# A graph transformer with linear attention and a mixture of experts on one core: the join of nodes that cross tiles multiplies in two reduced-precision parts, and the first attention's one-hots and slot gathers change their places in the queues

## The reference, cut to what matters

```python
for l in range(2):
    q = ((x @ Wq[l].T + bq[l]) * scaling).reshape(n, H, DH)      # H = 8, DH = 64
    k = (x @ Wk[l].T).reshape(n, H, DH)
    v = (x @ Wv[l].T).reshape(n, H, DH)
    scores = einsum('ehd,ehd->eh', q[tgt], k[srcidx])
    p = exp(scores - segment_max(scores, tgt)[tgt])
    w = p / (segment_sum(p, tgt)[tgt] + 1e-16)
    agg = segment_sum(w[:, :, None] * v[srcidx], tgt)
    x = batchnorm(x + agg.reshape(n, D) @ Wo[l].T + bo[l])
    x = batchnorm(x + relu(x @ W1[l].T + b1[l]) @ W2[l].T + b2[l])
```

## Time and profile before

| what | us |
|---|---|
| median of 3 runs | 3262.51 (3260.45 to 3280.92) |
| the profiled execution | 3271.22 |
| span of its instructions | 3269.9 |
| first attention, PE at work in it | about 508 to 1350 |
| first join, L1697 to the read back | 1381.5 to 1420.7 |
| second attention | about 1825 to 2507 |
| second join's matmuls | 2535.5 to 2565.8 |

### The profile page before, as it was taken

How to read it: one execution, slowest core, us unless ns; L and a number is a source line. 1 busy time by engine, 2 the same in 40 slices (tenths; PEclk the granted TensorE clock), 3 DMA queues, 4 the chain that set the end, 5 groups by cost and what they waited for, 6 DMA issues and landing times.

```text
span 3269.9 us, 78219 instructions
## 1 busy us (share of the span) xinstructions
PE 2847.2 (87%) x32206; PEld 1996.0 (61%) x32206; DVE 1677.8 (51%) x3300; ACT 1270.2 (39%) x3609; POOL 1098.5 (34%) x1109
## 2 busy tenths in 40 slices
PE   6999997999989998677799799889886785899998
PEld 5877875666666666355488566666664462444444
DVE  5237774555454544535513355555555357555554
ACT  3324444455544544212332355555554112222221
POOL 0000004666666555200001477777773001111100
PEclk8999998999999999788899899999998897899999
DMA  6542007888888888521024699999996221011100
GB/s 210 221 153 89 30 30 249 296 306 303 299 295 296 292 290 280 147 68 59 30 98 150 218 353 351 345 351 353 347 347 203 62 85 39 26 39 39 48 32 15
DMA packets 223590, 608.82 MB, mean 186 GB/s; under 512 B 37008, under 2 KB 43792, under 8 KB 223219
## 3 DMA queue, kind: packets, MB, share of 16 engines
q0 software_dynamic: 137088, 466.78, 40.6%
q1 hardware_dynamic: 86131, 136.85, 12.5%
HBM read 525.96 MB, written 103.29 MB: 192 GB/s over the span
## 4 chain that ended last, share of the span: by engine, by line
PE 66%; DMA 16%; DVE 6%; issue 6%; POOL 4%; ACT 2%; SPq 1%; POOLq 0%; DVEq 0%; ACTq 0%
PE ps L1106 8%; DMA stage<-Qd,segs 7%; PE ps L2320 5%; PE ps L1129 5%; PE ps L2341 5%; PE ps L555 4%; DMA Y<-KVd,srcE 4%; PE ps L556 4%; PE ps L557 4%; PE ps L1141 3%; PE ps L915 3%; PE ps L620 2%; PE ps L622 2%; PE ps L621 2%; PE ps L1697 2%
## 5 line engine op out<-in xcount | busy, mean ns | idle before, releaser
L1026 POOL DMA_INDIRECT Y<-KVd,srcE x449 | 438.1, 976 | 146.2 <-issue 107.0
L1106 PE MATMUL ps<-ident,Y 128*128 128x128 f32 x1796 | 287.1, 283 | 38.0 <-DMA Y<-KVd,srcE 30.5
L1301 ACT ACTIVATE stage<-ps,stage 128x128 f32<-128x128 f32 x832 | 293.2, 372 | 22.5 <-DVE stage L1213 20.6
L1026 POOL DMA_INDIRECT WA<-KVd,srcE x186 | 182.0, 979 | 330.9 <-PE ps L557 267.0
L1282 ACT ACTIVATE G<-ps 128x512 f32<-128x512 f32 x315 | 188.7, 600 | 255.5 <-PE ps L1106 254.4
L1282 ACT ACTIVATE work<-ps 128x512 f32<-128x512 f32 x309 | 185.6, 601 | 241.5 <-PE ps L1106 239.6
L555 PE MATMUL ps<-Wh,xs 128*128 128x512 f32 x600 | 238.8, 398 | 38.0 <-DVE xs L495 38.0
L1106 PEld LDWEIGHTS ps<-ident,Y 128*128 128x128 f32 x1796 | 200.6, 142 | 112.5 <-issue 70.3
L1035 POOL DMA_INDIRECT stage<-Qd,segs x104 | 105.9, 1018 | 472.0 <-DVE G L1247 292.2
L556 PE MATMUL ps<-Wl,xs 128*128 128x512 f32 x600 | 236.7, 394 | 0.0
L557 PE MATMUL ps<-Wh,xs 128*128 128x512 f32 x600 | 236.7, 394 | 0.0
(11 more groups left out here) (337 smaller groups left out, 6471.4 us busy)
## 6 DMA issues: line engine op xcount, KB each, us to landing
KVd<-stage SPq DMA_DIRECT2D x96, 256.0 KB, 2.0
aggd<-work SPq DMA_DIRECT2D x6, 2048.0 KB, 7.4
Qd<-stage SPq DMA_DIRECT2D x48, 256.0 KB, 2.0
G<-aggd SPq DMA_DIRECT2D x48, 256.0 KB, 2.7
Y<-KVd,srcE POOLq DMA_INDIRECT x449
Y<-in_x SPq DMA_DIRECT2D x4, 1536.0 KB, 14.7
G<-mixq SPq DMA_DIRECT2D x24, 256.0 KB
mixd<-rowsb SPq DMA_DIRECT2D x24, 256.0 KB
```

The source lines that it names most:

```text
L1026: pool.indirect_dma_start(out=kvs[a], out_offset=None, in_=KVd[l][:, :], in_offset=bass.IndirectOffsetOnAxis(ap=srcE[:, n:n + 1], axis=0)) ...
L1106: mm = pe.transpose(bank[:, k * P:(k + 1) * P], kvs[a][:, k * P:(k + 1) * P], ident[:, :])
L1301: last = act.activation(pT[g % len(pT)][:, P * i:P * (i + 1)], SC[g % 2][:, P * i:P * (i + 1)], ACT.Exp, bias=smin[:, t:t + 1], scale=-1.0 ...
```

## The change

In the join, each block of `part` is copied by ACT to an f32r tensor (`partH`), DVE subtracts that from the original into a second f32r tensor (`partL`, in place over `part`), the selector is written as f32r, and PE makes two f32r matmuls where it made one of f32. DVE's subtraction for block i-1 (`low`) stands behind the selector of block i. The selector ring stays at three.

In the first attention alone (`l == 0`): the one-hot of block b+3 is built in the odd g, where that of b+2 was; PE turns the one-hot of b+2 in the even g, between i = 1 and i = 2, where it did so after the odd g; DVE empties it at the end of the even g, where it did so at the end of the odd one; POOL issues the slot gather of an odd g behind the four K|V gathers of that g, where it stood ahead of them.

```diff
@@ turn_table: the order of the transposes
-                order += [("k", n) for n in range(4 * g + LOOK[l], min(4 * g + LOOK[l] + 4, ET))]
+                for i in range(4):
+                    order += [("k", n) for n in (4 * g + LOOK[l] + i,) if n < ET]
+                    if l == 0 and g % 2 == 0 and i == 1 and b + 2 < NJ:
+                        order.append(("hot", b + 2))
                 if g % 2 == 0 and b + 1 < NJ:
                     order.append(("q", b + 1))
-                if g % 2 and b + 2 < NJ:
+                if l == 1 and g % 2 and b + 2 < NJ:
                     order.append(("hot", b + 2))
@@ attend_pool
-                if g % 2 and j < NJ:
+                if l == 1 and g % 2 and j < NJ:
                     fetch_slots(j)
-                j = (g - 2 - AGG_AT) // 2
-                if g % 2 == AGG_AT % 2 and 0 <= j < NJ:
-                    scatter(j)
+                x = (g - 2 - AGG_AT) // 2
+                if g % 2 == AGG_AT % 2 and 0 <= x < NJ:
+                    scatter(x)
                 while at < ET and (at - KV) // 4 <= g - AGG_AT:
                     fetch(at)
                     at += 1
+                if l == 0 and g % 2 and j < NJ:
+                    fetch_slots(j)
@@ attend_pe
+                    if l == 0 and x == 0 and i == 1 and b + 2 < NJ:
+                        turn_hot(b + 2)
...
-                if x == 1 and b + 2 < NJ:
+                if l == 1 and x == 1 and b + 2 < NJ:
                     turn_hot(b + 2)
@@ attend_dve
             last.then_inc(filled, 1)
+            if l == 0:
+                one_hot(2)
...
-                if x == 1 and b + 2 < NJ:
+                if l == 1 and x == 1 and b + 2 < NJ:
                     one_hot(b + 2)
+                if l == 0 and x == 1 and b + 3 < NJ:
+                    one_hot(b + 3)
...
-                if x == 1 and b + 2 < NJ:
+                if x == l and b + 2 < NJ:
                     empty_hot(b + 2)
@@ join_dve
+            def low(i):
+                k, b = divmod(i, TB)
+                dve.wait_ge(part_hi, 8 * l + i + 1)
+                dve.tensor_tensor(partL[0:TP, i, :], part[k][:, b, :], partH[0:TP, i, :].bitcast(F32), ALU.subtract
+                                  ).then_inc(sel, 1)
+
...
                 dve.tensor_tensor(h8(part[k][:, b, :]), h8(part[k][:, b, :]),
-                                  fac[:, k, b, :].unsqueeze(2).to_broadcast([TP, H, DH]), ALU.mult)
+                                  fac[:, k, b, :].unsqueeze(2).to_broadcast([TP, H, DH]), ALU.mult).then_inc(scaled, 1)
                 if i >= 3:
                     dve.wait_ge(join_mm, 8 * l + i - 2)
-                dve.tensor_scalar(work[0:TP, i % 3, 0:ET], snB[0:TP, :], (nodeF, nodeL)[k][:, b:b + 1], None,
-                                  ALU.is_equal).then_inc(sel, 1)
+                dve.tensor_scalar(workR[0:TP, i % 3, 0:ET], snB[0:TP, :], (nodeF, nodeL)[k][:, b:b + 1], None,
+                                  ALU.is_equal)
+                if i:
+                    low(i - 1)
+            low(7)
@@ join_pe
-                    mm = pe.matmul(PS[q][0:TP, :], work[0:TP, i % 3, q * TP:(q + 1) * TP], part[k][:, b, :],
-                                   start=(i == 0), stop=(i == 7))
+                    rows = workR[0:TP, i % 3, q * TP:(q + 1) * TP]
+                    pe.matmul(PS[q][0:TP, :], rows, partH[0:TP, i, :], start=(i == 0), stop=False)
+                    mm = pe.matmul(PS[q][0:TP, :], rows, partL[0:TP, i, :], start=False, stop=(i == 7))
@@ join_act
+            for i in range(8):
+                act.wait_ge(scaled, 8 * l + i + 1)
+                act.activation(partH[0:TP, i, :], part[i // TB][:, i % TB, :], ACT.Copy).then_inc(part_hi, 1)
             act.wait_ge(join_mm, 8 * (l + 1))
```

More of the change, by code:

```diff
@@ L98, in build @@
         stage = sb("stage", [P, 4, 512])
+        with ExitStack() as under:
+            workR = under.enter_context(nc.sbuf_tensor("workR", [P, 3, 512], F32R))
         work = sb("work", [P, 3, 512])
@@ L784, in agg_tensors @@
                 lo = under.enter_context(nc.sbuf_tensor(f"aggL{l}", [P, 4, 512], F32R))
-            return hi, [lo, stageR]
+            with ExitStack() as under:
+                under.enter_context(nc.sbuf_tensor(f"under_part{l}", [P, 12800], F32))
+                part_lo = under.enter_context(nc.sbuf_tensor(f"partL{l}", [P, 8, 512], F32R))
+                part_hi = under.enter_context(nc.sbuf_tensor(f"partH{l}", [P, 8, 512], F32R))
+            return hi, [lo, stageR], part_hi, part_lo
         bgr = WA[:, 0].rearrange("p k o -> p (k o)")[:, 1200:1208]
         router = WA[:, 0].rearrange("p k o -> p (k o)")[:, 0:1200].rearrange("p (s e) -> p s e", s=6)
-        aggH, aggL = agg_tensors(0)
+        aggH, aggL, partH, partL = agg_tensors(0)
         Y, G = tensor("Y1", [P, 12800]), tensor("G1", [P, 16, 512])
@@ L1543, in build @@
         exp_arg, exp_made = sem("exp_arg"), sem("exp_made")
+        scaled, part_hi = sem("scaled"), sem("part_hi")
         sel, join_mm, join_ev, run_out = sem("sel"), sem("join_mm"), sem("join_ev"), sem("run_out")
@@ L1990, in build @@
         area.close()
-        aggH, aggL = agg_tensors(1)
+        aggH, aggL, partH, partL = agg_tensors(1)
         Y, G = tensor("Y2", [P, 12800]), tensor("G2", [P, 16, 512])
```

## The result

The changed kernel takes 3351.62 us (median of 4 runs, 3340.23 to 3360.63) against 3266.92 of the kernel before beside it (3260.45 to 3280.92): a ratio of 1.0245 [1.022, 1.027], slower by 85 us. The profiled execution took 3348.75 us, its span 3347.4, the mean granted clock over it 0.928 for 0.942.

The account below looks back on a forecast made before the run. PE was taken to set the pace, its idle time ended by late K|V gathers. First attention -57 + 85, joins -23, sum +5 us on 3262.5: forecast 3267 us, range 3198 to 3310.

Parts of the forecast that it names:

- second rival: First attention: slot gather lands slower behind four K|V gathers; 3312 us at 6.2 us, over 1% slower from 5.9; chance 0.2.
- The join: Both joins: f32r matmuls replace f32 ones, 18.8 us for 30.4 in each; -23 us for two (-20 to -25).
- I let all 46.3 us go ... Together -57: First attention: all PE waits for K|V gathers vanish, with 11 us for modelled record ends; -57 us (-46 to -60).
- The slot gather's wait: First attention: gather starts 2.6 us after turn_k, lands in 5.3 with 3.6 available; PE waits 1.7 us nearly every period.
- The rule of the Trainium skill: Slot gather: about 2.0 us plus bytes over 436 GB/s, 3.6 us with issuing; the +85 us would be 0.
- 50 x 1.7 = +85: First attention: PE's new wait for the slot gather, 1.7 us in 50 periods, +85 us (ends +17 and +150).
- The first rival: First attention: slot gather lands early; 3200 us at 3.95 us, over 1% faster from 4.5 us downward; chance 0.28.
- the third: Joins: DVE's subtraction sets the pace or the lower clock stays; -11 us at most, 3279 or 3290 us; chance 0.07.

Follow-up runs that it names:

- e3: The changed kernel with the slot gather back ahead of the odd group's K|V gathers, the one-hots still a group sooner: 3174.5 us, 0.9700 of before.
- e1: The kernel before with the join's change alone, nothing of the attention's: 3246.4 us, 0.9929 of before.
- e8: The changed kernel with the one-hots where they were before, the slot gather still behind the K|V gathers: 3347.5 us, 1.0229 of before.
- e4: The changed kernel with the last three K|V gathers of every first-attention group released two tiles sooner: 3330.2 us, 1.0180 of before.
- e7: The changed kernel with the slot gather between the third and fourth K|V gather of the odd group: 3241.0 us, 0.9913 of before.
- e6: The changed kernel with the queries' turn on PE and its emptying on ACT moved to the odd group, behind i = 1: 3189.7 us, 0.9749 of before.
- e9: The changed kernel with the slot gather behind the first K|V gather of the odd group: 3190.2 us, 0.9773 of before.
- e5: The changed kernel with 16 unused identity transposes ahead of PE's wait for each slot gather in the first attention: 3300.0 us, 1.0099 of before.
- e10: e3 with the same 16 unused identity transposes ahead of the queries' transpose, where PE waits for nothing: 3252.6 us, 0.9953 of before.

## Why the prediction was wrong

Predicted 3267 us (3198 to 3310); measured 3351.6, beyond the slow end. The direction is the second rival's, but not its condition: that rival asked for landings of over 5.9 us and had 3312 us at 6.2. The landings measured, 5.7 us in the mean, lie within the forecast's own 4.6 to 5.9, for which it gave 3232 to 3297 us. So the time was missed with the landing almost right.

**The join: right.** From the scaling factor's being ready to ACT's first copy out I read 20.9 and 19.7 us in the two joins for 31.7 and 31.6 before, 22.8 us together, for 23 predicted; 20.6 and 18 by the runs. In the first join 14 matmuls start 0.43 us apart at the lower clock, for the 13 foreseen, and DVE was not the bound: PE is busy 17.92 of 17.96 us.

**"I let all 46.3 us go ... Together -57": right in kind, too small in size.** The K|V waits are gone. e3 against e1 makes it -72 us by the medians, (16.00 - 14.64) x 50 = 68 by the periods, beyond the -46 to -60 of the prediction. The waits of e1 for K|V are 41.6 us, the modelled ends 59 x 0.16 = 9, the clock from 0.99 to 1.00 some 7; the last 11 to 15 us were not taken apart. The error of 15 us is to the fast side and hid a part of the miss. The reason given, that the sooner one-hots free these gathers, is one of two: the new order does it by itself (e8).

**The slot gather's wait: the mechanism right, the size short.** The start after `turn_k`, 2.6 us, was met in the example; in the trace's starts it is 2.6 and 2.9 us by turns but for three of 4.2, 2.8 in the mean. Its landing takes 5.7 us in the mean of all periods for the 5.3 taken. That lies inside the bounds; together they make 2.4 us of waiting for 1.7: 50 x 2.4 = 120 us for +85. The reason given for the start was half right: the `turn_k` of i = 1 holds the fourth gather up by 0.18 us in every second period and not at all in the others; the rest is the V sum's release, the `turn_k` of i = 0 and POOL's issue time of 1.24 us for each gather (e4). The rule of the Trainium skill, page "DMA: Bandwidth & Descriptors", section "Anatomy of one DMA", by which the gather would have been in time, did not hold here: the estimate worked out from it was 3.6 us with the issuing, and the landings in the trace take 5.7 us in the mean, the shortest 4.0.

**What failed: the term "50 x 1.7 = +85" priced a wait of PE at its own length.** A term was missing, what the wait does to the clock (the 2.4 GHz level against 1.2 behind it). With waits of 2.4 us in every period the granted clock of the first attention is 0.93, and filling them with idle work gives 52 us back by the medians, 50 x (18.21 - 17.00) = 60 by the periods. I priced a lower clock for the join and not for the attention. The earlier trace rows show no price for a short wait, since PE had stood almost idle for some 20 us there. But the trace of before has waits of `turn_q` for the slot gather in the second attention, and behind some of them the clock is down. Of the next two the first runs at a clock of 1.00 in the 3 us that follow, the second at 0.50:

```profile
1982.52 0.66 PE L1098 MATMUL ps<-ident,stage 128*128 128x128 f32 x4 [2.32 <-DMA stage<-Qd,segs]
...
2240.36 0.90 PE L1098 MATMUL ps<-ident,stage 128*128 128x128 f32 x3 [1.86 <-DMA stage<-Qd,segs]
```

So it was to be seen that such waits can cost clock, not how often. It is no constant price: with waits of 1.1 us (e7) the clock stays at 0.99. What decides between two waits of like length stays open.

The sum with what the runs give: -72 + 120 + 52 to 60 - 21 = +79 to +87, against +85 measured. The miss of 85 us against the forecast (3351.6 for 3267) is, term by term: the clock 52 to 60, the length of the waits 35, the joins 2, and some 4 because the kernel before measured 3266.9 beside the change and not 3262.5; less the 15 of the K|V waits. Without the clock's part the measured time would lie inside the range.

The first rival fails with its landing (5.7 us, not under 4.5); the third is not borne out, since the joins give what was forecast.

## What to carry to other kernels

When a transfer with little slack is moved behind others in an issuing engine's list, count that engine's time for each of them (here 1.24 us) from the event that releases the first; then ask where the consumer's list first needs it, since moving that point (e6) or the transfer (e3, e9) repairs the same loss. Price a new wait of TensorE, where TensorE sets the pace, at its own length and at the slower clock behind it: look in the trace of before what granted clock stands behind pauses of its length. A change in two parts may hold a gain and a larger loss, and the parts need not add: here the sooner one-hots were worth -72 us in the old order and nothing in the new one, and the order cost 101 us without them and 177 with them.

## What the runs showed of the hardware

Added work on TensorE made the kernel 52 us faster (e5), since the mean granted clock rose from 0.93 to 1.00; the same work cost 78 us where TensorE had no pause (e10). With a pause of 2.4 us in each period the mean granted clock was 0.93, and in the example the transposes behind a pause of 3.02 us ran at the level of 1.2 GHz; with pauses of 1.1 us (e7) it was 0.99. In the changed kernel the clock fell behind 33 of 50 pauses, once behind one of 1.68 us, while it stayed up behind another of 2.42 us. Gathers of 128 rows of 2 KB behind four gathers of 128 rows of 4 KB landed 5.7 us after their issue in the mean (4.0 to 8.0); one after 4.4 us without a gather took 3.95 us.
